# Fourteen products of zeros on TensorE between the state stages of the two batches

## The reference, cut to what matters

```python
xz = jnp.einsum('bld,ed->ble', x, W_in)
xp, z = jnp.split(xz, 2, axis=-1)
xc = silu(conv_b + sum(xpad[:, k:k + l, :] * conv_w[:, k] for k in range(d_conv)))
dbc = jnp.einsum('ble,fe->blf', xc, W_x)          # 128 rows of dt, 16 of Bm, 16 of Cm
dt, Bm, Cm = ...
delta = softplus(jnp.einsum('blr,er->ble', dt, W_dt) + b_dt)
dA = jnp.exp(delta[..., None] * A)
dBx = delta[..., None] * Bm[:, :, None, :] * xc[..., None]
h = dA_t * h + dBx_t                              # a scan over the 512 tokens
y = jnp.einsum('bles,bls->ble', hs, Cm) + xc * Dp
return jnp.einsum('ble,de->bld', y * silu(z), W_out)
```

## Time and profile before

| | |
|---|---|
| median of three runs | 850.93 us |
| profiled execution, own time | 852.66 us |
| its span, first to last instruction | 850.7 us |
| around the span | 1.96 us |
| TensorE busy | 763.7 us (90%) |
| VectorE busy | 561.1 us (66%) |
| ScalarE busy | 407.7 us (48%) |
| GpSimd busy | 254.3 us (30%) |
| mean granted TensorE clock | 0.967 |

### The profile page before, as it was taken

One profiled execution on the slowest core, in us unless ns is written; L12 is line 12 of the kernel. 1 busy time (PEld: TensorE's weight loads), 2 busy tenths in 40 slices (PEclk: granted clock), 3 DMA queues, 4 the chain that ended last, 5 costly groups with the idle time before them and its releaser, 6 DMA issues.

```text
span 850.7 us, 10806 instructions
## 1 busy us (share of the span) xinstructions
PE 763.7 (90%) x3862; PEld 527.4 (62%) x3862; DVE 561.1 (66%) x984; ACT 407.7 (48%) x600; POOL 254.3 (30%) x189
## 2 busy tenths in 40 slices
PE   4899989986779799999999998997899998788997
PEld 3587565653326366667876776774457775445776
DVE  4444699999969999963464446358765646844443
ACT  3344797666456787732232233441575421373221
POOL 0000059985428787850994000001000010000000
PEclk9999989999988999999998999999999999899999
DMA  9300022222101222217001000033000340000000
GB/s 279 115 2 1 2 62 75 74 75 62 50 26 56 64 71 65 79 38 229 2 1 22 1 1 0 13 110 94 10 1 1 80 115 30 2 27 1 1 1 25
DMA packets 30591, 41.75 MB, mean 49 GB/s; under 512 B 3753, under 2 KB 19955, under 8 KB 30515
## 3 DMA queue, kind: packets, MB, share of 16 engines
q1 hardware_dynamic: 29290, 40.91, 16.4%
q10 hardware_dynamic: 1252, 0.19, 0.2%
HBM read 36.73 MB, written 4.26 MB: 48 GB/s over the span
## 4 chain that ended last, share of the span: by engine, by line
PE 66%; DVE 15%; issue 9%; ACT 6%; DMA 2%; POOL 1%; SPq 0%; DVEq 0%; ACTq 0%
PE PS L495 35%; PE PS L835 7%; PE PS L573 3%; DVE PS L1938 3%; PE PS L1040 2%; PE PS L1023 2%; PE PS L801 2%; DVE shared L1946 2%; PE PS L616 2%; PE PS L722 1%; ACT shared L1547 1%; PE PS L453 1%; PE PS L819 1%; PE PS L904 1%; DMA shared<-in_L_ffn_W_dram 1%
## 5 line engine op out<-in xcount | busy, mean ns | idle before, releaser
L2254 POOL TENSOR_TENSOR shared<-shared,route 128x1024 f32<-128x1024 f32 x64 | 151.5, 2370 | 78.0 <-DVE shared L1946 72.3
L495 PE MATMUL PS<-xnT,work_r 128*128 128x512 f32 (+1 forms) x624 | 156.7, 402 | 0.0
L495 PE MATMUL PS<-xnT,weights_r 128*128 128x256 f32 (+1 forms) x732 | 155.3, 359 | 0.5 <-issue 0.4
L1946 DVE TENSOR_TENSOR_SCAN shared<-shared,PS 128x512 f32<-128x512 f32 x128 | 148.7, 1204 | 0.0
L495 PEld LDWEIGHTS PS<-xnT,weights_r 128*128 128x128 f32 x732 | 114.9, 191 | 33.3 <-issue 20.0
L495 PEld LDWEIGHTS PS<-xnT,work_r 128*128 128x128 f32 (+1 forms) x624 | 114.1, 188 | 28.7 <-issue 1.5
L835 PE MATMUL PS<-shared,cf 128*128 128x512 f32 x256 | 123.1, 604 | 0.0
L1705 DVE TENSOR_TENSOR gated<-gated,PS 128x512 f32<-128x512 f32 (+1 forms) x52 | 35.6, 685 | 106.4 <-ACT gated L1205 106.4
L1205 ACT ACTIVATE gated<-PS 128x512 f32<-128x512 f32 (+1 forms) x52 | 31.1, 598 | 143.8 <-PE PS L495 138.9
L1489 ACT ACTIVATE shared<-shared,cols 128x512 f32<-128x512 f32 x128 | 83.7, 712 | 24.2 <-DVE shared L1946 20.5
L495 PE MATMUL PS<-weights_r,work_r 128*128 128x256 f32 (+1 forms) x624 | 89.4, 293 | 1.4 <-DVE work_r L1712 1.1
(11 more groups left out here) (222 smaller groups left out, 1092.2 us busy)
## 6 DMA issues: line engine op xcount, KB each, us to landing
route<-scratch_c SPq DMA_DIRECT2D x64, 256.0 KB, 3.2
shared<-in_L_ffn_W_dram SPq DMA_DIRECT2D x3, 1024.0 KB, 8.9
scratch_k<-shared SPq DMA_DIRECT2D x12, 128.0 KB
scratch_q<-shared SPq DMA_DIRECT2D x12, 128.0 KB
shared<-scratch_k SPq DMA_DIRECT2D x8, 192.0 KB
shared<-scratch_q SPq DMA_DIRECT2D x8, 192.0 KB
mamba_w<-in_L_ffn_w_dram SPq DMA_DIRECT2D x2, 704.0 KB, 5.2
beside<-in_L_ffn_w_dram SPq DMA_DIRECT2D x2, 704.0 KB, 7.5
```

The source lines that it names most:

```text
L495: last = nc.tensor.matmul(o, lhs[l], rhs[r], start=(start and i == 0), stop=(stop and i == 2))
L1946: v.tensor_tensor_scan(hst[:, (t % 2 * 2 + j) * T:(t % 2 * 2 + j + 1) * T], decay[t % D_SLOTS][:, j * T:(j + 1) * T], products[:, j * T:(j ...
L2254: nc.gpsimd.tensor_tensor(hc[:, u * 2 * T:(u + 1) * 2 * T].rearrange("p (c t) -> p c t", c=2), hst[:, (t % 2) * 2 * T:(t % 2 + 1) * 2 * T] ...
```

## The change

TensorE's opening of batch 1 changes. The wait on `mul` (batch 0's last row of Bm has been read, so bank 0 is free) moves in front of the wait on `dtT` (the copy of dt). Between the two waits stand 14 products of zeros into bank 0. `step_output(0)` writes the same bank afterwards.

```diff
 RING = 2
+JOINT_PRODUCTS = 14
 START_PRODUCTS, TAIL_PRODUCTS = 8, (13, 18)
...
                     step_input(3).then_inc(s["dt"], 1)
                     row_input(3).then_inc(s["bc"], 1)
+                    pe.wait_ge(s["mul"], HEAD + 2 * STEPS)
+                    self.idle_products(B_BANK, JOINT_PRODUCTS)
                     pe.wait_ge(s["dtT"], 2)
-                    pe.wait_ge(s["mul"], HEAD + 2 * STEPS)
                     step_output(0)
                     step_output(1)
                     add_state(STEPS - 1, 0)
```

## The result

The median is 854.38 us over 15 runs (852.25 to 857.72) against 851.39 us of the kernel before over 15 (847.14 to 854.82): +2.99 us by the medians, and a ratio of 1.0042 (+3.6 us) with an interval of 1.0026 to 1.0057, so +2.2 to +4.9 us. The forecast was 853.8, +2.91. Of all the executions behind this document one, of the kernel before, took 901.27 us at a mean clock of 0.83, and it enters no ratio. The profiled execution of the changed kernel took 854.01 us, with a span of 852.2. Lines behind the change are one or two higher in it: L512 is now L513, L819 L820, L842 L843, L1433 L1435, L1906 L1908, L1938 L1940.

What follows compares the result with a forecast made beforehand. The chain of row inputs, L842, L1433 and L1906 was taken to bound batch 1's start. Products of 3.01 us less 0.10 hidden gave 2.91, and 850.93 + 2.91 = 853.8 us, range 851.3 to 856.9.

Steps and rivals of the forecast that it cites:

- What bounds the place: Batch 1's opening: row inputs, L842, L1433 and L1906 form one chain, so what delays L1906 delays all later steps.
- The length of the products: Batch 1's opening: fourteen products hold the array for 14 x 0.215 = 3.01 us at a granted clock of 1.00.
- What hides them: Wait for the copy of dt before L842: bounds nothing or 0.69 us hidden; 0.10 us taken, leaving 2.91.
- The wait on mul: Moved up in batch 1's opening: L1938 ends 6.7 us before TensorE gets there, so it costs nothing.
- The gap and the clock: TensorE's idle time between add_state(31) and step_output(2): stays 4.2 us, clock falls to 0.50 again, steps lose 0.64 us again.
- a sign of being wrong: VectorE's steps 0 to 5 taking another time than 3.42 us each plus 0.64 in all.
- the clock comes out better: Rival behind the gap: low stretch ends earlier against VectorE's steps or falls away, +2.27 us, 853.2 us; chance 0.10.
- TensorE as the bound of the first steps: Rival: clock returns later than step 3's broadcast, VectorE waits, +4.6 us, 855.5 us; chance 0.16 including one low stretch more.
- the half clock: Rival in batch 1's opening: products run at clock 0.50 and take 6.0 us, 856.9 us; chance 0.03.
- Low stretches in later stages: Later TensorE-bound stages: 3.4 us at half clock costs 1.7; one less gives +1.2, chance 0.08, one more +4.6.

## Why the prediction was right

*What bounds the place.* Right. L842's delay goes one for one to L1906 and the steps: +2.93 for 14 products, and back the same way, -2.52 for three row inputs less.

*The length of the products.* 3.01 us were expected, 3.02 measured, at a clock of 1.00.

*What hides them.* 0.10 was taken out of 0 to 0.69; the trace has 0.09. Two other kernels bear it out: the exchange alone costs 0.06, the products behind the copy's wait cost 0.08 more than in front of it. In the changed kernel L843's weight load starts at 244.76, 0.21 us ahead of its matmul and under the last product:

```profile
244.76 0.41 PEld L843 LDWEIGHTS PS<-shared 128*128 128x128 f32 x2
```

The Trainium skill's sentence on weight loads that run ahead of running matmuls ("TensorE: Matmul & The Clock Gate", Architectural detail) fits this row, and L843's 1.88 us in place of 1.98.

*The wait on mul.* It was put at nothing. Without products the exchange costs 0.06 us.

*The gap and the clock.* The gap stayed at 4.21 us and the clock fell, as expected. (The row of 248 to 249 that the prediction reads as 0.50 shows a mean of 0.66, since the fall lies inside it, at 248.3.) Wrong was the step from there to the steps' loss: I took the same gap to mean the same low stretch, and so put all of the 2.91 on the end. In fact the low stretch was shorter in all five traces with products, and the steps lost 0 where the kernel before lost 0.45 to 0.65 us in its three. The prediction had named this as a sign of being wrong (steps 0 to 5 in another time than 3.42 each plus 0.64), and the sign came. So did another: the stages behind did not keep their lengths. It is the rival "the clock comes out better" with its own price, 0.64, to which I gave 0.10; by it the median would have been 853.2. Whether the products bring it about or chance does stays open.

*Luck in the number.* By the traces the net cost at step 5 is 2.93 less 0.45 to 0.65, some 2.3 to 2.5 us. The medians, +2.99 and, again, +2.9 us, don't tell that from 2.9: the intervals are +2.2 to +4.9 and +0.1 to +4.3 us, and runs of one kernel lie 7.7 us apart. That the first came within 0.1 us of the forecast is luck. What is shown is the 2.93 us at the place.

*The rivals that ended slower.* TensorE as the bound of the first steps did not come (0.0 us of waiting in the row of L1940), and neither did the half clock. Low stretches in later stages moved both ways, at 1.9 us for 3.4 us less at half clock between the transposes at 427 and 490, near the 1.7 that was used. They make up part of the spread of the runs, not all of it: over the 33 executions of the kernel before beside the first experiments (846.39 to 855.83 us) time and mean clock have a correlation of -0.70.

## What to carry to other kernels

Ask of work put into a schedule to keep an engine busy whether it stands in the idle time or ahead of it: up to VectorE's first multiplication of the steps the same fourteen products cost 2.9 us ahead of the chain's first matmul, 1.4 behind the gap, and nothing in the gap. A wait that is written in the program is not a wait that is spent: here L842 started 0.86 us behind the row input ahead of it, which is the distance that two records have anyway. Where the products do cost their length, real work stands in the same place, and moving that off the chain won 2.5 us there and, by two ratios with wide intervals, 2.1 to 2.4 in the total. And compare a clock between kernels only over several executions of each: one pair showed a difference of 0.65 us that three traces of the kernel before put at 0.45 to 0.65, and that other kernels without products ahead of the gap did not always have.

## What the runs showed of the hardware that I had not expected

With TensorE's gap the same 4.2 us, the clock's fall and the length of the low stretch behind it were not the same: 13.6 us in four of six traces without products ahead of it, 6.8 and 3.4 in the other two, 3.4 and 3.4 in five of five with them. With the gap filled down to 1.19 us the clock did not fall there, and fell at 257 instead, at the second of two idle times of 1.89 and 1.97 us with a product pair between them. In the kernel before the clock stayed low from 248.3 to 262.0, though TensorE was busy for 10.23 of the 12 us from 249 to 261. The clock's rule of the Trainium skill ("TensorE: Matmul & The Clock Gate", What's actually happening), that activity releases the throttle, agrees with the filled gap; by itself it does not say why that busy stretch stayed low. That work ahead of an unfilled gap shortens the low stretch is not shown: the counts lean that way, and the cause stays open.
